# Attention output stored without padding, its denominators inverted where they are used and spread by TensorE

## The chip, the core and the metric

The kernel runs on one core of a Trainium2 chip. The metric is the device time of one execution in microseconds (us). The kernel before takes 3326.37 us, the median of three runs (3324.26 to 3327.92).

## The reference, cut to what matters

Eight batches of 512 tokens of width 256 pass through a cross-attention to a context of 1601 tokens, then through a block of causal self-attention and eight routed experts. The change touches how the output of both attentions is normalized:

```python
x = x + xattn(layernorm(x), ctx, ctx, Wq, bq, Wk, bk, Wv, bv, Wo, bo)
# inside xattn, 16 heads of 16 columns:
scores = einsum('bqhd,bkhd->bhqk', q, k) * scale
attn = softmax(scores, axis=-1)
out = einsum('bhqk,bkhd->bqhd', attn, v).reshape(B, -1, DIM)
return out @ Wo.T + bo
# then, with x <- layernorm(x):
h = x + attention(rmsnorm(x, g1), wq, wk, wv, wo)     # causal, 512 tokens, rotary
y = h + moe(rmsnorm(h, g2), w_router, wg, wu, wd)     # 8 experts, top 2
```

## The kernel before, in words

The kernel is a sequence of stages. Each stage is a block in which every engine runs its own list of instructions. Engines wait for each other through semaphores, and a barrier of all engines stands between two stages. The stages are: `prepare_weights`; `project_inputs`; `attention` over the context (names with `att_cross_`); `invert_denominators`; `project_self` (names with `slf_`); `attention` over the tokens themselves (`att_self_`); `invert_denominators` again; `finish_self` (names with `fin_`); then routing, scattering, the experts and the final sum.

In `attention`, a unit is four heads of one batch, so there are 32 units in each attention. A head takes 32 rows of the 128 partitions of `out_buf`: 16 rows of output, one row with the softmax denominator (row `HD` of the head, because the values carry a column of ones), and 15 unused rows. SyncE sends each unit's 128 rows to DRAM as one transfer (`send_out`, L597).

`invert_denominators` reads the 128 denominator rows back from DRAM (L856), takes their reciprocal on VectorE (L864) and writes them to the DRAM tensor `inverse` (L858). `load_attention_out` (L875, L878), called by the two later stages, then gathers a batch with six transfers: four bring two row groups for each half of `oT`, and two read `inverse` so that each head's row is repeated for its 16 partitions. VectorE multiplies the two in `divide` (L1040 and L1252), and TensorE multiplies the result with the output weights (`out_product`, L990 and L1222).

`project_self` and `finish_self` are software pipelines over the eight batches, written by `turns`: a list of parts with lags for each engine. In step t, an engine runs each part of its list in the order written, for batch t minus the part's lag. So the order within a step is fixed and an engine that waits in one part does not go on to the next.

In `project_self` the parts are: on VectorE `subtract_high` of k (L1078), `residual` (L1046, with the sums of the first norm), `divide` (L1040), `rope(0)` (L1070, L1071, which reads the products of q), `layer_norm` (L1052, L1056), `rms_inverse`, `subtract_high` of q and `rope(1)` (k). On TensorE they are `turn_rows` (L999, a transposition of the rows that ScalarE scaled after the layer norm), `out_product` (L990), `q_products` (L1008), `v_product` (L1022) and `k_products` (L1008). The products of q and k share PSUM banks, so `k_products` waits until `rope(0)` has read those of q. `residual` also waits until the rows of the batch before have landed in DRAM (`rows_sent`).

In `finish_self` every batch also loads two tensors of rows (L1209) and stores two (L1298, L1303). GpSimd's `weigh` (L1328) waits until the stored rows of the batch before have landed.

## Time and profile before

| what | value |
|---|---|
| median of three runs | 3326.37 us |
| the profiled execution, its own time | 3328.94 us |
| its span in the profile | 3327.4 us |
| busy PE, VectorE, ScalarE, GpSimd | 81%, 53%, 44%, 15% |
| mean granted TensorE clock | 0.905 |

The profile divides the span into stages that do not overlap, since a barrier ends each. A stage is as long as its own slowest chain, so a mean over the span tells little: TensorE is 81% busy over the whole, but 75% in `project_self` (180.91 us of 240) and 43% in `finish_self` (75.83 us of 175). The rows below are read stage by stage.

### The profile page before, as it was taken

What the parts mean: (1) busy time and instruction counts of PE and PEld (TensorE: products, weight loads), DVE (VectorE), ACT (ScalarE), POOL (GpSimd) and SP (SyncE); (2) the same over time, 40 slices, a digit from 0 to 9 for tenths busy, and PEclk for the clock granted to TensorE, in tenths of its full rate; (3) what the DMA queues carried; (4) which work ended last, traced back from release to release, by engine and by line L of the source; (5) the groups of instructions that cost most, each with busy time, mean ns of one, the idle gap of its engine ahead of it and who ended that gap; (6) DMA issues with size and microseconds to landing.
All of it is one profiled execution on the core that took longest, in us unless ns stands there. A gap on an engine that the chain in (4) does not pass through costs nothing. (4 is left out here: it accounts for less than half of the span.)

```text
span 3327.4 us, 54791 instructions
## 1 busy us (share of the span) xinstructions
PE 2706.5 (81%) x14654; PEld 1326.7 (40%) x14655; DVE 1767.8 (53%) x2838; ACT 1460.1 (44%) x2951; POOL 488.0 (15%) x638
## 2 busy tenths in 40 slices
PE   7996899999999999999948778888341299999980
PEld 5662232323232323233235434443231177777760
DVE  5665776767676767677346556664222022222223
ACT  2331576767676767677713335555110022222210
POOL 2444000000000000000014411110133400000006
PEclk9996899999999999999979979999665599999995
DMA  7888444444444444443045556654444211001115
GB/s 239 266 286 155 79 72 77 71 77 71 76 72 75 73 73 75 72 74 58 22 133 195 178 131 142 142 141 105 145 144 152 95 33 33 32 32 32 32 46 182
DMA packets 317615, 347.91 MB, mean 105 GB/s; under 512 B 37328, under 2 KB 262776, under 8 KB 317312
## 3 DMA queue, kind: packets, MB, share of 16 engines
q1 hardware_dynamic: 285584, 291.53, 38.6%
q0 software_dynamic: 11392, 37.76, 3.6%
q10 hardware_dynamic: 20464, 16.40, 1.6%
q8 instruction: 96, 1.57, 0.2%
q14 instruction: 79, 0.65, 0.1%
HBM read 206.22 MB, written 138.57 MB: 104 GB/s over the span
## 5 line engine op out<-in xcount | busy, mean ns | idle before, releaser
L727 DVE TENSOR_REDUCE att_cross_neg_max<-att_cross_ps_s 128x1 f32<-128x802 f32 x1024 | 965.6, 988 | 357.3 <-PE att_cross_ps_s L644 355.6
L798 ACT ACTIVATE att_cross_probs<-att_cross_ps_st 128x512 f32<-128x512 f32 (+1 forms) x1664 | 901.4, 599 | 401.0 <-PE att_cross_ps_st L663 388.4
L663 PE MATMUL att_cross_ps_st<-att_cross_q_pack,att_cross_k_pack 99*128 99x512 bf16 (+1 forms) x1664 | 575.3, 391 | 42.7 <-issue 33.8
L644 PE MATMUL att_cross_ps_s<-att_cross_k_pack,att_cross_q_pack 96*128 96x401 bf16 x2048 | 548.2, 351 | 70.1 <-DVE att_cross_neg_max L727 29.5
L678 PE MATMUL att_cross_ps_o<-att_cross_probs,att_cross_v_tiles 128*32 128x512 f32 (+1 forms) x3328 | 453.4, 618 | 1.0
L644 PEld LDWEIGHTS att_cross_ps_s<-att_cross_k_pack,att_cross_q_pack 96*128 96x128 bf16 x2048 | 177.1, 100 | 420.6 <-DVE att_cross_neg_max L727 204.5
L663 PEld LDWEIGHTS att_cross_ps_st<-att_cross_q_pack,att_cross_k_pack 99*128 99x128 bf16 (+1 forms) x1664 | 163.1, 100 | 421.2 <-ACT att_cross_probs L798 293.1
L727 DVE TENSOR_REDUCE att_self_neg_max<-att_self_ps_s 128x1 f32<-128x128 f32 (+3 forms) x512 | 236.5, 489 | 162.7 <-PE att_self_ps_s L647 159.7
L798 ACT ACTIVATE att_self_probs<-att_self_ps_st 128x256 f32<-128x256 f32 (+3 forms) x512 | 208.5, 441 | 156.8 <-PE att_self_ps_st L666 150.8
L1756 DVE COPY moe_hiddenT<-moe_ps_h 128x256 f32<-128x256 f32 x142 | 60.3, 424 | 297.2 <-PE moe_ps_h L1666 297.2
L644 PE MATMUL att_self_ps_s<-att_self_k_pack,att_self_q_pack 96*128 96x128 bf16 (+3 forms) x512 | 160.6, 316 | 56.4 <-DMA att_self_q_pack<-q_parts 25.1
L1720 ACT ACTIVATE moe_silu<-moe_ps_g 128x352 f32<-128x352 f32 x142 | 65.8, 463 | 301.0 <-PE moe_ps_u L1658 301.0
L1676 PE MATMUL moe_ps_y<-top_wd_sb,moe_hiddenT 128*128 (+1 forms) x852 | 196.0, 379 | 1.2 <-DVE moe_hiddenT L1757 1.2
L1658 PE MATMUL moe_ps_g<-top_wg_sb,moe_rowsT 128*128 x568 | 192.8, 462 | 0.0
L1658 PE MATMUL moe_ps_u<-top_wu_sb,moe_rowsT 128*128 x568 | 192.0, 461 | 0.0
L769 POOL CAST att_cross_neg_max_parts<-att_cross_neg_max_merged 128x16 bf16<-128x16 f32 x32 | 6.1, 192 | 1245.1 <-DVE att_cross_neg_max_merged L718 1245.1
L1676 PEld LDWEIGHTS moe_ps_y<-top_wd_sb,moe_hiddenT 128*128 128x128 f32 (+1 forms) x852 | 161.6, 190 | 35.3 <-issue 1.5
L663 PE MATMUL att_self_ps_st<-att_self_q_pack,att_self_k_pack 99*128 99x256 bf16 (+3 forms) x512 | 157.4, 310 | 17.3 <-DMA att_self_q_pack<-att_self_neg_max_rows 15.2
L1750 DVE TENSOR_TENSOR moe_hidden<-moe_ps_u,moe_silu 128x352 f32<-128x352 f32 x142 | 73.5, 517 | 159.3 <-ACT moe_silu L1720 159.3
L1828 POOL DMA_INDIRECT comb_row<-out_sorted,comb_index x64 | 62.1, 970 | 622.6 <-DVE comb_index L1838 603.4
L1658 PEld LDWEIGHTS moe_ps_u<-top_wu_sb,moe_rowsT 128*128 128x128 f32 x568 | 108.5, 191 | 60.7 <-issue 1.0
L678 PEld LDWEIGHTS att_cross_ps_o<-att_cross_probs,att_cross_v_tiles 128*32 128x32 f32 (+1 forms) x3328 | 66.6, 108 | 151.9 <-ACT att_cross_probs L798 113.9
(208 smaller groups left out, 2910.6 us busy)
## 6 DMA issues: line engine op xcount, KB each, us to landing
att_cross_k_pack<-k_parts SPq DMA_DIRECT2D x192, 200.1 KB, 9.5
v_rows<-in_v_pad SPq DMA_DIRECT2D x24, 1024.0 KB, 4.5
att_cross_v_tiles<-v_rows SPq DMA_DIRECT2D x32, 768.0 KB
k_parts<-in_part SPq DMA_DIRECT2D x72, 256.0 KB, 4.0
in_rows<-in_ctx_dram SPq DMA_DIRECT2D x24, 512.0 KB, 4.8
att_cross_q_pack<-q_parts SPq DMA_DIRECT2D x192, 64.0 KB, 10.0
att_self_k_pack<-k_parts SPq DMA_DIRECT2D x192, 64.0 KB, 3.2
att_self_q_pack<-q_parts SPq DMA_DIRECT2D x192, 64.0 KB, 3.6
```

Source lines behind the costliest of these rows:

```text
L644: last = nc.tensor.matmul(ps_s[bank][:, n, 0:w], qp[v.buf][0:SROWS, j, q * P:(q + 1) * P], kp[v.buf][0:SROWS, j, s:s + w], start=True, sto ...
L663: mm = nc.tensor.matmul(ps_st[bank_of_step[s]][0:rows, q0:SEQ], kp[u.buf][0:MROWS, j, t * P:t * P + rows], qp[u.buf][0:MROWS, j, q0:SEQ], ...
L678: nc.tensor.matmul(ps_o[j * VW:(j + 1) * VW, q0:SEQ], va[u.vbuf][0:rows, t, j * VW:(j + 1) * VW], pr[0:rows, (u.odd * STEPS + t * GH + j) ...
L727: nc.vector.tensor_reduce(nmax[v.odd][:, col, half:half + 1], ps_s[bank][:, 0:len(spans), 0:spans[0][1]], AX.XY, ALU.max, negate=True).the ...
L769: link(nc.gpsimd.tensor_copy(nm_parts[:, 0, :], full))
L798: nc.scalar.activation(pr[0:rows, (u.odd * STEPS + s) % RING, q0:SEQ], ps_st[bank_of_step[s]][0:rows, q0:SEQ], ACT.Exp).then_inc(exp_done, 1)
L1658: last = nc.tensor.matmul(ps[half][:, 0:HHALF], xT[t.par][:, i, :], wt[:, bass.ds(at, HHALF)], start=(i == 0), stop=(i == KC - 1))
L1676: last = nc.tensor.matmul(ps_y[:, :], hT[half][0:CW[c], c, :], wd[0:CW[c], bass.ds(at, DIM)], start=(half == 0 and c == 0), stop=(half == ...
L1720: nc.scalar.activation(sil[half][:, :], ps_g[half][:, 0:HHALF], ACT.Silu).then_inc(sil_ready, 1)
L1750: nc.vector.tensor_tensor(h[half][:, :], ps_u[half][:, 0:HHALF], sil[half][:, :], ALU.mult)\
L1756: nc.vector.tensor_copy(hT[half][:, 0:CH - 1, :], ps_h[half][:, 0:CH - 1, :])
L1828: pool.indirect_dma_start(out=r[g][k][c][:, :], out_offset=None, in_=out_sorted, in_offset=bass.IndirectOffsetOnAxis(ap=index[g][:, c, k:k ...
```

## The change

The rows of `out_rows` are stored without padding. For each unit, SyncE sends four transfers of 16 rows and one of the 4 denominator rows, to a DRAM tensor of their own, `den_rows`. The two stages `invert_denominators` are gone. `load_attention_out` becomes two transfers a batch: the 256 rows of output and the 16 rows of denominators.

In `project_self` and `finish_self`, VectorE inverts the 16 denominator rows (`invert`, a new part ahead of `residual`). TensorE multiplies a constant 16 by 256 matrix of zeros and ones with them (`spread_inverse`, a new part at the head of its list), so that each head's row stands on its 16 partitions in PSUM. `divide` reads this PSUM tile. In `project_self` the tile is `ps_o`, the one that `out_product` writes afterwards, so `spread_inverse` waits until `residual` of the batch before has read it, and `divide` moves behind `rope(0)`. In `finish_self` the tile is one of its own, `ps_b`. The constants become 256 columns wider.

```diff
 def send_out(v):
     sp.wait_ge(o_read, v.n + 2)
-    sp.dma_start(out_rows[v.n, :, :], ob[v.odd][:, :]).then_inc(o_sent[v.odd], 16)
+    for j in range(GH):
+        sp.dma_start(out_rows[v.batch, v.rows.start + j * HD:v.rows.start + (j + 1) * HD, :],
+                     ob[v.odd][j * VW:j * VW + HD, :]).then_inc(o_sent[v.odd], 16)
+    sp.dma_start(den_rows[v.batch, v.heads, :], ob[v.odd][HD:P:VW, :]).then_inc(o_sent[v.odd], 16)
...
+def load_attention_out(eng, out_rows, den_rows, oT, den, b, arrived):
+    eng.dma_start(oT[:, :, :], out_rows[b, :, :].rearrange("(c p) n -> p c n", p=P)).then_inc(arrived, 16)
+    eng.dma_start(den[:, :], den_rows[b, :, :]).then_inc(arrived, 16)
...
 # project_self, TensorE
+def spread_inverse(b):
+    pe.wait_ge(inv_ready, b + 1)
+    pe.wait_ge(x1_ready, b + 1)
+    for c in range(KC):
+        last = nc.tensor.matmul(ps_o[:, c * 2:(c + 1) * 2, :].rearrange("p t d -> p (t d)"),
+                                keep["spread"][0:HEADS, c * P:(c + 1) * P], inv[:, :],
+                                start=True, stop=True)
+    last.then_inc(spread, 1)
-turns(pe, batches, ((1, turn_rows), (0, out_product), (1, q_products), (1, v_product),
+turns(pe, batches, ((0, spread_inverse), (1, turn_rows), (0, out_product), (1, q_products), (1, v_product),
                     (1, k_products)))
 # project_self, VectorE
 def divide(b):
+    dve.wait_ge(spread, b + 1)
+    nc.vector.tensor_tensor(on[:, :, :], oT[:, :, :],
+                            ps_o[:, :, :].rearrange("p (c t) d -> p c (t d)", c=KC),
+                            ALU.mult).then_inc(on_ready, 1)
+def invert(b):
     dve.wait_ge(att_in, (b + 1) * ATT_LOADS)
-    nc.vector.tensor_tensor(on[:, :, :], oT[:, :, :], inv[:, :, :], ALU.mult).then_inc(on_ready, 1)
+    dve.wait_ge(spread, b)
+    nc.vector.reciprocal(inv[:, :], den[:, :]).then_inc(inv_ready, 1)
-turns(dve, batches, ((3, lambda b: subtract_high(1, b)), (1, residual), (0, divide),
-                     (2, lambda b: rope(0, b)), (1, layer_norm), (1, rms_inverse),
+turns(dve, batches, ((3, lambda b: subtract_high(1, b)), (0, invert), (1, residual), (2, lambda b: rope(0, b)),
+                     (0, divide), (1, layer_norm), (1, rms_inverse),
                      (2, lambda b: subtract_high(0, b)), (2, lambda b: rope(1, b))))
 # finish_self, TensorE and VectorE
-turns(pe, batches, ((2, turn_rows), (0, out_product), (2, router)))
+turns(pe, batches, ((0, spread_inverse), (2, turn_rows), (0, out_product), (2, router)))
-turns(dve, batches, ((1, residual), (0, divide), (1, mean_square), (1, rms_inverse),
+turns(dve, batches, ((0, invert), (1, residual), (0, divide), (1, mean_square), (1, rms_inverse),
                      (3, take_logits)))
```

VectorE, the body of the loop of `project_self` before, from the second instruction on. A row is a line of the code, the operation, what it writes and reads, and its shape.

```order
L1046 TENSOR_TENSOR slf_x<-slf_ps_o,slf_x_biased 128x1024
L173 BN_STATS slf_norm_stats<-slf_x 128x6 x4
L176 BN_AGGR slf_norm_mean_var<-slf_norm_stats 128x2 x4
L1040 TENSOR_TENSOR slf_o_normed<-slf_oT,slf_inv_rows 128x1024
L1070 TENSOR_TENSOR slf_rope_cos<-slf_ps_a,top_keep_constants 128x512
L1071 TENSOR_TENSOR slf_rope_sin<-slf_ps_b,top_keep_constants 128x512
L1052 RECIPROCAL slf_norm_std_inv<-slf_norm_std 128x4
L1056 TENSOR_SCALAR slf_h<-slf_x,slf_norm_mean_var,slf_norm_std_inv 128x256 x4
```

The same place in the changed kernel:

```order
L1031 RECIPROCAL slf_inverse<-slf_denominators 16x512
L1037 TENSOR_TENSOR slf_x<-slf_ps_o,slf_x_biased 128x1024
L173 BN_STATS slf_norm_stats<-slf_x 128x6 x4
L176 BN_AGGR slf_norm_mean_var<-slf_norm_stats 128x2 x4
L1061 TENSOR_TENSOR slf_rope_cos<-slf_ps_a,top_keep_constants 128x512
L1062 TENSOR_TENSOR slf_rope_sin<-slf_ps_b,top_keep_constants 128x512
L1024 TENSOR_TENSOR slf_o_normed<-slf_oT,slf_ps_o 128x1024
L1043 RECIPROCAL slf_norm_std_inv<-slf_norm_std 128x4
L1047 TENSOR_SCALAR slf_h<-slf_x,slf_norm_mean_var,slf_norm_std_inv 128x256 x4
```

A reciprocal of 16 rows of 512 has come in ahead of the residual, and the division has moved from ahead of the rope rows to directly ahead of the layer norm (L1043). It now reads `slf_ps_o`, a PSUM tile.

TensorE, the body of the loop of `project_self` before:

```order
L999 MATMUL slf_ps_t<-top_keep_constants,slf_x_rms 128x128 x8
L990 MATMUL slf_ps_o<-top_keep_WoT,slf_o_normed 128x256 x8
L1008 MATMUL slf_ps_a<-slf_xT,top_keep_wq 128x512 x4
L1008 MATMUL slf_ps_b<-slf_xT,top_keep_wq_rot 128x512 x4
L1022 MATMUL slf_ps_t<-top_keep_wv,slf_xT 128x256 x8
L1008 MATMUL slf_ps_a<-slf_xT,top_keep_wk 128x512 x4
L1008 MATMUL slf_ps_b<-slf_xT,top_keep_wk_rot 128x512 x4
```

And in the changed kernel:

```order
L965 MATMUL slf_ps_o<-slf_inverse,top_keep_constants 128x512 x2
L983 MATMUL slf_ps_t<-top_keep_constants,slf_x_rms 128x128 x8
L974 MATMUL slf_ps_o<-top_keep_WoT,slf_o_normed 128x256 x8
L992 MATMUL slf_ps_a<-slf_xT,top_keep_wq 128x512 x4
L992 MATMUL slf_ps_b<-slf_xT,top_keep_wq_rot 128x512 x4
L1006 MATMUL slf_ps_t<-top_keep_wv,slf_xT 128x256 x8
L992 MATMUL slf_ps_a<-slf_xT,top_keep_wk 128x512 x4
L992 MATMUL slf_ps_b<-slf_xT,top_keep_wk_rot 128x512 x4
```

Two matmuls (L965) stand at the head of the body, that is, behind the products of k of the step before.

## Rows read from the trace of the kernel before

**Rows 1.** Windows: stretch, length, busy PE, PEld, DVE, ACT, POOL, clock, DMA, GB/s.

```profile
1678.00:1918.00 240.00, 180.91 (x576) 106.99 (x576) 134.77 (x290) 70.92 (x129) 95.29 (x64) 0.90 0.53 175
2337.00:2512.00 175.00, 75.83 (x320) 64.65 (x320) 45.80 (x112) 24.97 (x49) 43.09 (x40) 0.65 0.45 144
```

**Rows 2.** Timeline (start, length, instruction, [idle before]) between the cross attention and `project_self`.

```profile
1663.89 0.33 SPq L597 DMA_DIRECT2D out_rows<-att_cross_out_buf  x1
...
1668.14 0.34 SPq L856 DMA_DIRECT2D inv_cross_den<-out_rows  x1
1670.84 3.35 DVE L864 RECIPROCAL inv_cross_inv<-inv_cross_den 128x512 f32<-128x512 f32 x1 [50.27 <-DMA inv_cross_den<-out_rows]
...
1677.28 0.91 DVE L1032 MEMSET slf_v_pad<- 128x1024 f32 x1 [3.10 <-PEq L65]
1678.34 1.29 SPq L875 DMA_DIRECT2D slf_oT<-out_rows  x2
```

**Rows 3.** Timeline of SyncE between the self attention and `finish_self`.

```profile
2327.37 0.35 SPq L856 DMA_DIRECT2D inv_self_den<-out_rows  x1
...
2336.80 1.26 SPq L875 DMA_DIRECT2D fin_oT<-out_rows  x2
```

**Rows 4.** Timeline of one step in the middle of `project_self`.

```profile
1795.15 1.23 DVE L1046 TENSOR_TENSOR slf_x<-slf_ps_o,slf_x_biased 128x1024 f32<-128x1024 f32 x1 [2.08 <-DMA h_rows<-slf_h]
...
1798.24 1.19 DVE L1040 TENSOR_TENSOR slf_o_normed<-slf_oT,slf_inv_rows 128x1024 f32<-128x1024 f32 x1
...
1799.35 0.68 DVE L1070 TENSOR_TENSOR slf_rope_cos<-slf_ps_a,top_keep_constants 128x512 f32<-128x512 f32 x1
...
1801.74 0.17 DVE L1052 RECIPROCAL slf_norm_std_inv<-slf_norm_std 128x4 f32<-128x4 f32 x1
...
1801.88 3.70 PE L1008 MATMUL slf_ps_a<-slf_xT,top_keep_wk 128*128 128x512 f32 x8 [1.67 <-DVE slf_rope_sin L1071]
...
1805.42 3.60 PE L1008 MATMUL slf_ps_b<-slf_xT,top_keep_wk_rot 128*128 128x512 f32 x8
...
1810.47 1.09 PE L999 MATMUL slf_ps_t<-top_keep_constants,slf_x_rms 128*128 128x128 f32 x8 [1.46 <-ACT slf_x_rms L1103]
...
1814.85 3.60 PE L1008 MATMUL slf_ps_a<-slf_xT,top_keep_wq 128*128 128x512 f32 x8
...
1816.98 1.22 DVE L1078 TENSOR_TENSOR slf_roped_rest<-slf_roped,slf_roped_part 128x1024 f32<-128x1024 f32 x1 [4.86 <-ACT slf_roped_part L1124]
...
1821.72 3.62 PE L1022 MATMUL slf_ps_t<-top_keep_wv,slf_xT 128*128 128x256 f32 x16
```

**Rows 5.** Timeline of `project_self`, its first division and products, first and last transposition.

```profile
1690.07 1.22 DVE L1040 TENSOR_TENSOR slf_o_normed<-slf_oT,slf_inv_rows 128x1024 f32<-128x1024 f32 x1 [11.60 <-DMA slf_inv_rows<-inverse]
...
1691.35 6.51 PE L990 MATMUL slf_ps_o<-top_keep_WoT,slf_o_normed 128*128 128x256 f32 x16 [28.21 <-DVE slf_o_normed L1040]
...
1712.05 1.97 PE L999 MATMUL slf_ps_t<-top_keep_constants,slf_x_rms 128*128 128x128 f32 x8 [14.19 <-ACT slf_x_rms L1103]
...
1882.69 1.09 PE L999 MATMUL slf_ps_t<-top_keep_constants,slf_x_rms 128*128 128x128 f32 x8 [0.76 <-ACT slf_x_rms L1103]
```

**Rows 6.** The division of `finish_self`: count, duration in ns (min/median/max), first and last start.

```profile
L1252 DVE TENSOR_TENSOR fin_o_normed<-fin_oT,fin_inv_rows x8: 1224/1226/2485, 2349.9 to 2475.5; 128x1024 f32<-128x1024 f32 x8
```

**Rows 7.** Timeline of `finish_self`, one load of the attention's output.

```profile
2351.32 1.40 SPq L875 DMA_DIRECT2D fin_oT<-out_rows  x2
...
2362.56 1.23 DVE L1252 TENSOR_TENSOR fin_o_normed<-fin_oT,fin_inv_rows 128x1024 f32<-128x1024 f32 x1 [4.12 <-DMA fin_inv_rows<-inverse]
```

**Rows 8.** Waits of `finish_self`: us in total, times, longest.

```profile
POOL fin_h_normed L1328 <- DMA hn_rows<-fin_h_normed: 84.8, 6, 20.1
```

**Rows 9.** The page's DMA issues: count, KB each, median us to landing.

```profile
in_rows<-in_ctx_dram SPq DMA_DIRECT2D x24, 512.0 KB, 4.8
```

**Rows 10.** Waits of SyncE in the self attention.

```profile
SPq L588 <- PE att_self_ps_o L678: 137.6, 28, 15.6
```

**Rows 11.** Timeline of SyncE in the self attention, one unit's store.

```profile
2112.01 0.38 SPq L597 DMA_DIRECT2D out_rows<-att_self_out_buf  x1
```

More of the change, by code:

```diff
@@ L448, in project_inputs, with attention @@
         p.clear()
-def attention(nc, q_parts, k_parts, v_rows, out_rows, kv, causal, keep, units, beside=None):
+def attention(nc, q_parts, k_parts, v_rows, out_rows, den_rows, kv, causal, keep, units, beside=None):
     tiles = [(t, min(P, kv - t * P)) for t in range(-(-kv // P))]
@@ L531, in __init__ @@
                 self.rows = slice(g * GR, (g + 1) * GR)
+                self.heads = slice(g * GH, (g + 1) * GH)
                 self.columns = slice(g * GH * VW, (g + 1) * GH * VW)
@@ L624, in _ @@
                 for k in range(2):
-                    sp.wait_ge(o_sent[k], 16 * (units // 2 + 1))
+                    sp.wait_ge(o_sent[k], OSENT * (units // 2 + 1))
             @block.tensor
@@ L912, in project_self @@
         on_ready = p.sem("on_ready")
+        inv_ready = p.sem("inv_ready")
+        spread = p.sem("spread")
         xb_ready = p.sem("xb_ready")
@@ L1183, in finish_self @@
         on_ready = p.sem("on_ready")
+        inv_ready = p.sem("inv_ready")
+        spread = p.sem("spread")
         o_done = p.sem("o_done")
@@ L1216, in _, with spread_inverse @@
                 pe.sem_inc(turned, 1)
+                def spread_inverse(b):
+                    pe.wait_ge(inv_ready, b + 1)
+                    pe.wait_ge(on_ready, b + 1)
+                    for c in range(KC):
+                        last = nc.tensor.matmul(ps_b[:, c, :],
+                                                keep["spread"][0:HEADS, c * P:(c + 1) * P], inv[:, :],
+                                                start=True, stop=True)
+                    last.then_inc(spread, 1)
                 def out_product(b):
@@ L1250, in divide, with invert @@
                 def divide(b):
+                    dve.wait_ge(spread, b + 1)
+                    nc.vector.tensor_tensor(on[:, :, :], oT[:, :, :], ps_b[:, :, :], ALU.mult).then_inc(on_ready, 1)
+                def invert(b):
                     dve.wait_ge(att_in, (b + 1) * ATT_LOADS)
-                    nc.vector.tensor_tensor(on[:, :, :], oT[:, :, :], inv[:, :, :], ALU.mult).then_inc(on_ready, 1)
+                    dve.wait_ge(spread, b)
+                    nc.vector.reciprocal(inv[:, :], den[:, :]).then_inc(inv_ready, 1)
                 def residual(b):
@@ L1867 @@
              ("cos_k", SEQ), ("sin_k", SEQ), ("iota_left", EXPERTS), ("iota_tile", 96), ("iota_count", 64),
-             ("lt8", EXPERTS * EXPERTS))
+             ("lt8", EXPERTS * EXPERTS), ("spread", DIM))
 def shape_constants():
@@ L1890, in shape_constants @@
         "lt8": np.tile((e[None, :] < e[:, None]).astype(np.float32).reshape(1, -1), (P, 1)),
+        "spread": (np.arange(DIM)[None, :] // HD == i[:, None]).astype(np.float32),
     }
@@ L1951, in build @@
     v2_rows = dram("v2_rows", [batches, SEQ, HEADS * VW])
[L1952 to L1953 removed]
+    out2_rows = dram("out2_rows", [batches, DIM, SEQ])
+    den2_rows = dram("den2_rows", [batches, HEADS, SEQ])
     tokens = batches * SEQ
```

68 lines of the change are left out of this document (19 added, 49 removed).

## The prediction

> **What bounds the kernel now.** I read the stages first. `project_self` and `finish_self` are two stretches of the span between barriers [rows 1], so what the change does there adds up with what it does at the two joins. The reader should see two different stages. In the first, TensorE is busy 181 of 240 us at a granted clock of 0.90. In the second it is busy 76 of 175 us at 0.65, with the 16 DMA engines at 0.45. Then I read the two joins [rows 2, 3], and last the timeline of one step of each pipeline.
>
> A step of `project_self` [rows 4]: the transposition for batch t-1 starts at 1810.47, its products of v at 1821.72, and the products of k run from 1801.88 to 1809.02. So TensorE goes round almost without a pause: it waits 1.5 us for the scaled rows and 1.7 us for VectorE's rope. From the first transposition to the last are 170.64 us for seven steps [rows 5], 24.4 us each. The point to see is what runs beside k: the division is done at 1799.4, the rope at 1801.8, and the layer norm starts at 1801.74. VectorE's and ScalarE's 8.7 us from there to the transposition lie under the 7.1 us of the products of k.
>
> A step of `finish_self` takes (2475.5 - 2349.9) / 7 = 17.9 us from division to division [rows 6]. All eight divisions end a wait for a load. One load, alone on the queues, takes 2362.56 - 2351.32 = 11.2 us [rows 7], though it moves 1 MB. GpSimd waits 84.8 us in six times for stored rows to land [rows 8].
>
> **Joins.** Both inversion stages go. At the first, the next stage's memsets can start where L856 stands (1668.14) and its first load 1.06 us later, against 1678.34 [rows 2]: 9.1 us less. At the second 9.4 us [rows 3]. Sum -18.6. Against it, the last unit's store is now five issues instead of one. At 0.38 us an issue [rows 11] that is 1.5 us later, for two stages +3.0. **Joins: -15.6 us**, bounds -18.6 (the four earlier ones hidden in the wait for the landing) and -12 (each issue doubled by its address arithmetic).
>
> In the attentions themselves, a unit gets four more issues on SyncE, 1.5 to 3 us. SyncE waits 137.6 us in 28 times for the values' buffer [rows 10], 4.9 us a unit, so they are hidden in the self attention, whose units are the short ones. If the issues took over 1.2 us each, the loads would come late. I take 0.
>
> The constants grow by 128 KB. By 512 KB in 4.8 us [rows 9] that is at most 1.2 us ahead of the first matmul. It is one more stream among others there. **+0.5 us.**
>
> **The steps of `project_self`.** This is the term that decides. `divide` for batch t now waits for `spread_inverse`, which stands on TensorE behind the products of k of the step before. The layer norm for t-1 stands behind `divide`, and the transposition for t-1 waits for the layer norm. What ran beside k now runs after it. I call D the start of a division, and work out the next D from rows 4.
>
> - D to the transposition: the division 1.2, then from the layer norm's start to the transposition 8.7, less the 0.8 us in which ScalarE was busy with a cast that is now long done: D + 9.1.
> - TensorE from there: products of v at + 11.25, hence k possible at + 14.7: D + 23.8.
> - k also needs the rope of q. VectorE reaches it after `subtract_high` at transposition + 6.5 (D + 15.6, 1.2 us), the new reciprocal, and the residual with its sums (3.1 us up to the rope). The reciprocal of 128x512 took 3.35 us [rows 2]. No row has 16 partitions. Its bounds are 0.2 (the 128x4 one took 0.17 us, rows 4) and 3.35, and I take 3.35, since the columns are the same 512. The rope then starts at D + 23.2, and k 2.5 us later, D + 25.7.
> - k takes 7.0 until TensorE is free, D + 32.7. The spread is two matmuls of 512 columns in fp32. Eight records of such are 3.6 us, and four matmuls are eight records, so two are 1.8 to 1.9. Next D = D + 34.6.
>
> The loads for batch t+1 are issued at D + 1.3 and needed at D + 16.8, and the stored rows have 11 us more than before, so no transfer ends a wait here. A step is 34.6 us instead of 24.4. The first transposition: the division for batch 0 came 11.7 us after the first load (1690.07, rows 5). Now 5.5 us of load, 3.35 of reciprocal and 3.6 of a spread at the low clock make 12.7, and the second round has the reciprocal and the spread in it again: 37.5 us after the first load instead of 33.7, +3.8. Six steps of 34.6 and a last one of 22.0, which has no division behind it, make 229.6 against 170.64: +59.0. Together **+62.8 us**. With the reciprocal at its lower bound k starts at D + 23.8 and the term is +51.
>
> **The clock.** TensorE now stands idle from the end of the spread to the transposition, 9.2 us in each step. After the idle 14.2 us before 1712.05 the granted clock was at its lower level: the transposition took 1.97 us instead of 1.09, and the cold product of 16 records 6.51 us [rows 5]. In `finish_self`, with pauses of similar length, the mean clock is 0.65 [rows 1]. Up to 9.2 us of each step at half speed would cost 4.6 us less what waits for the rope anyway (1.9), six times: 16 us, or 28 us if it falls on k. Nothing here shows a pause of 9 us behind 25 us of dense work. I take **+8 us**, bounds 0 and +28.
> The Trainium skill (TensorE: Matmul & The Clock Gate, section HAM oscillation) says that idle waits between groups of matmuls send the clock back to half in each group. By that rule the term would stand at the upper part of its range. The rows of `finish_self` agree with it.
>
> **The steps of `finish_self`.** The load becomes 0.5 MB in two transfers. The nearest row is 512 KB in 4.8 us [rows 9], so 11.2 becomes about 6. Behind it come the reciprocal, 3.35, and a spread at the low clock, 3.6, which stand in the chain from load to division: 13 us against 11.2 + 1.2. By this path alone nothing is won. But a step takes 17.9 us, since stored rows land late and the next loads wait for them behind GpSimd. A sixth of the bytes of a step goes (3.0 MB to 2.5 MB), and that shortens each landing. I take 16 us a step, **-14 us** for seven. Bounds: 13 us a step, -35, and 2 us a step more, +14.
> The Trainium skill (DMA: Bandwidth & Descriptors, section Queues, rings and completion order) says that a transfer runs on as many engines as divide the slowest dimension of both sides. The old gather's source had 4 there, the repeated one 8, the new load has 128. By that rule the old loads sat on four engines and held up every store behind them, and the term would be nearer to -35. No view of the trace before splits the engines.
>
> **Sum.** -15.6 + 0.5 + 62.8 + 8 - 14 = +41.7 us. The profiled execution took 3328.94 us (its span 3327.4 and 1.5 around it), 2.6 above the median, and would become 3370.6. On the median, 3326.4 + 41.7 = 3368.1 us.
>
> **The rivals.**
> 1. The steps of `project_self` do not grow. Then the joins and `finish_self` remain: -15.6 + 0.5 - 14 + 4 = -25, 3301 us. It needs the division to find its spread ready while k still runs. For it speaks that VectorE has 10 us of idle time in a step, so that 4 us more work fit. Against it stands TensorE's list: two matmuls cannot pass eight. A chance of 0.08. This is the one on the other side, and it decides from the point at which the spread comes before k.
> 2. The loads were the bound of everything: `finish_self` at -35, the reciprocal cheap (-11.8) and the clock unmoved: 41.7 - 21 - 11.8 - 8 = +1, 3327 us. A chance of 0.05.
> 3. The clock falls in every step and `finish_self` gains nothing: 41.7 + 20 + 14 = +76, 3402 us. A pause of 9 us in each step speaks for it, TensorE's 70% of busy time in a step against it. A chance of 0.08.
> 4. The change does not do what it says, the loads being no faster. The 0.5 MB then takes 11 us as before, and in `finish_self` 7 us of reciprocal and spread come on top of a step: 7 x 5 instead of -14: +91, 3417 us. Rows 9 speak against it. A chance of 0.03.
>
> My forecast, slower by the stretched step, has 0.76. The range is 3338 to 3398 us. The lower end is reached with the reciprocal cheap and `finish_self` at -26 together with a smaller clock term, the upper with the clock term at +28 and `finish_self` at -4. About 0.2 is left out on both sides. A difference of 0.2% (6.7 us) is what a measurement of this kernel can tell from none. Faster: rival 1 and a little of rival 2, 0.09. Same: the rest of rival 2 and a very cheap case of the forecast, 0.04. Slower: 0.87.
>
> **What would show it.** In the changed kernel, transpositions (L983) about 34.6 us apart, the two spread matmuls directly behind the products of k, a division that ends a wait for the spread in each step, and TensorE idle for 9 us behind it. `project_self` 300 to 315 us long. The joins 9 us shorter each. Divisions of `finish_self` about 16 us apart, their loads landing in about 6 us. The reciprocal of 16 rows at 3.35 us. The prediction is wrong if the transpositions stay within 27 us of each other, or if `finish_self` falls below 140 us.

## Result: 14 us slower, a third of what was forecast

The changed kernel takes 3338.6 us (median of five runs, 3336.3 to 3344.7), the kernel before, run beside it, 3324.3 us. The ratio is 1.005, with a 95% interval of 1.0035 to 1.0064, which is 12 to 21 us: slower by 14 us by the medians. The forecast was 42 us slower. The sign held, and so did the mechanism of `project_self`. Two terms of the sum were mis-sized, `project_self` by 15 us and `finish_self` by 17 us. One execution of `norm_and_store_first` (11080 us) and one of the kernel before beside it (6451 us) stand far outside all others and are left out of the ratios.

The profiled execution took 3344.66 us (span 3343.1), 6 us above the median. The stages are cut at the same instructions in both traces: the joins from the last copy of an attention's output to the next stage's first load, `project_self` from its first load to its last transposition, the self attention from its first load to its last copy, `finish_self` from its first load to the first reduction of the routing.

| part | before | after | difference | forecast |
|---|---|---|---|---|
| two joins | 15.05 + 14.04 | 8.12 + 6.54 | -14.4 | -15.6 |
| `project_self` | 204.35 | 259.97 | +55.6 | +62.8 + 8 |
| self attention | 403.11 | 412.49 | +9.4 | 0 |
| `finish_self` | 176.06 | 144.67 | -31.4 | -14 |
| all else | | | -3.5 | +0.5 |
| span | 3327.4 | 3343.1 | +15.7 | +41.7 |

The table compares one execution with one. The parts that the change decides, the joins, `project_self` and `finish_self`, give +9.8 us together.

The first join, SyncE in the timeline of the changed kernel:

```profile
1662.46 1.71 SPq L600 DMA_DIRECT2D out_rows<-att_cross_out_buf  x4
1664.21 0.52 SPq L602 DMA_DIRECT2D den_rows<-att_cross_out_buf  x1
...
1669.97 0.39 SPq L849 DMA_DIRECT2D slf_oT<-out_rows  x1
```

Against [rows 2] the inversion is gone and the first load stands 6.9 us closer to the last output. The five issues take 2.3 us instead of 0.33, 0.4 us more than forecast.

One step of `project_self`, TensorE and then VectorE, in the changed kernel:

```profile
1768.91 1.96 PE L983 MATMUL slf_ps_t<-top_keep_constants,slf_x_rms 128*128 128x128 f32 x8 [7.65 <-ACT slf_x_rms L1094]
1770.66 5.33 PE L974 MATMUL slf_ps_o<-top_keep_WoT,slf_o_normed 128*128 128x256 f32 x16
1775.83 3.60 PE L992 MATMUL slf_ps_a<-slf_xT,top_keep_wq 128*128 128x512 f32 x8
1779.27 3.60 PE L992 MATMUL slf_ps_b<-slf_xT,top_keep_wq_rot 128*128 128x512 f32 x8
1782.70 3.62 PE L1006 MATMUL slf_ps_t<-top_keep_wv,slf_xT 128*128 128x256 f32 x16
1786.15 3.60 PE L992 MATMUL slf_ps_a<-slf_xT,top_keep_wk 128*128 128x512 f32 x8
...
1793.11 1.98 PE L965 MATMUL slf_ps_o<-slf_inverse,top_keep_constants 16*128 16x512 f32 x4
```

```profile
1761.30 1.22 DVE L1024 TENSOR_TENSOR slf_o_normed<-slf_oT,slf_ps_o 128x1024 f32<-128x1024 f32 x1 [9.51 <-PE slf_ps_o L965]
...
1762.68 1.38 DVE L1047 TENSOR_SCALAR slf_h<-slf_x,slf_norm_mean_var,slf_norm_std_inv 128x256 f32<-128x256 f32 x4
...
1776.55 3.33 DVE L1031 RECIPROCAL slf_inverse<-slf_denominators 16x512 f32<-16x512 f32 x1
...
1795.13 1.22 DVE L1024 TENSOR_TENSOR slf_o_normed<-slf_oT,slf_ps_o 128x1024 f32<-128x1024 f32 x1 [9.65 <-PE slf_ps_o L965]
```

This is the chain that the prediction described, and it answers to [rows 4]. VectorE waits 9.65 us for the spread, then TensorE waits 7.65 us for the layer norm behind the division. From division to division are 33.8 us (34.1 in the last steps, 24.4 before). The windows show the clock: half of full speed for 10.2 us that begin within the pause, full speed in the rest of the step.

```profile
1764.30:1774.50 10.20, 5.59 (x18) 4.86 (x19) 5.67 (x16) 4.38 (x9) 4.43 (x2) 0.52 1.01 364
1774.50:1798.40 23.90, 20.59 (x59) 10.75 (x58) 12.92 (x23) 4.35 (x8) 7.16 (x6) 0.99 0.12 42
```

In `finish_self` the divisions are 14.7 us apart (17.9, [rows 6]), and one step reads:

```profile
2456.15 1.22 DVE L1256 TENSOR_TENSOR fin_o_normed<-fin_oT,fin_ps_b 128x1024 f32<-128x1024 f32 x1 [2.79 <-PE fin_ps_b L1217]
...
2458.25 0.34 SPq L850 DMA_DIRECT2D fin_denominators<-den_rows  x1
...
2463.82 3.34 DVE L1261 RECIPROCAL fin_inverse<-fin_denominators 16x512 f32<-16x512 f32 x1 [3.42 <-DMA fin_denominators<-den_rows]
2467.21 3.77 PE L1217 MATMUL fin_ps_b<-fin_inverse,top_keep_constants 16*128 16x512 f32 x4 [2.41 <-DVE fin_inverse L1261]
2471.02 1.22 DVE L1256 TENSOR_TENSOR fin_o_normed<-fin_oT,fin_ps_b 128x1024 f32<-128x1024 f32 x1 [2.79 <-PE fin_ps_b L1217]
```

That is a closed loop through one buffer: division, loads, reciprocal, spread, division. What surprised is how fast the rest became. Stored rows land in 4.5 and 5.1 us, before in 8.2 and 9.4 (count, KB each, median us from issue to landing, over the whole stage; first before, then after):

```profile
y_rows<-fin_y ACTq DMA_DIRECT2D x8, 512.0 KB, 8.2
hn_rows<-fin_h_normed ACTq DMA_DIRECT2D x8, 512.0 KB, 9.4
```

```profile
y_rows<-fin_y ACTq DMA_DIRECT2D x8, 512.0 KB, 4.5
hn_rows<-fin_h_normed ACTq DMA_DIRECT2D x8, 512.0 KB, 5.1
```

The DMA view shows what changed on the engines. Each fence is one view of 40 slices, busy tenths of the 16 engines above and GB/s below; first before (2455 to 2476), then after (2456 to 2476):

```profile
DMA  2225749999983201113459999975542222222210
GB/s 98 101 94 109 142 154 365 279 252 326 351 263 101 72 20 16 43 23 113 179 168 324 328 377 380 376 250 199 195 172 109 101 96 103 101 101 94 98 49 0
```

```profile
DMA  0006199999999999999000000000000006499999
GB/s 0 0 0 18 33 330 385 387 383 356 361 377 393 357 385 387 379 391 360 27 0 0 0 0 0 0 0 0 0 0 0 0 10 92 61 326 365 377 391 373
```

Before, both loads in the view end in a tail with the share at 0.2 and some 100 GB/s, a quarter of the 385 GB/s of full stretches, and ahead of the second tail stand 1.6 us at 0.5 and 172 to 199 GB/s. After, all of that is gone. The prediction had only the mean share of 0.45, which is 0.44 after.

### The profile page after: what moved, and what is told of

It is laid out like the page before. It is cut to its first block and busy times, and to the rows that moved or that the text cites. A ratio compares the mean times of both kernels' runs of the same rounds, so it can differ in the third digit from the quotient of the medians.

```text
span 3343.1 us, 55461 instructions
## 1 busy us (share of the span) xinstructions
PE 2764.0 (83%) x14718; PEld 1351.7 (40%) x14719; DVE 1795.0 (54%) x2852; ACT 1461.1 (44%) x2951; POOL 483.6 (14%) x638
## 5 line engine op out<-in xcount | busy, mean ns | idle before, releaser
L668 PE MATMUL att_cross_ps_st<-att_cross_q_pack,att_cross_k_pack 99*128 99x512 bf16 (+1 forms) x1664 | 574.2, 390 | 43.6 <-issue 34.6
## 6 DMA issues: line engine op xcount, KB each, us to landing
att_cross_q_pack<-q_parts SPq DMA_DIRECT2D x192, 64.0 KB, 10.2
```

Source lines behind the costliest of these rows:

```text
L668: mm = nc.tensor.matmul(ps_st[bank_of_step[s]][0:rows, q0:SEQ], kp[u.buf][0:MROWS, j, t * P:t * P + rows], qp[u.buf][0:MROWS, j, q0:SEQ], ...
```

## Experiments on the step of `project_self`

My theory: nothing runs beside k, because the layer norm stands behind a division that waits for the spread. The rivals: the spread's place behind k on TensorE, or the added work itself. Each ratio is to runs of the kernel before on the same chip, whose medians lie between 3316 and 3324 us. Where a kernel was executed once, only its profile is read, and no ratio is given.

**Layer norm ahead of the division (`dve_norm_first`).**

```diff
-  (0, divide), (1, layer_norm), (1, rms_inverse),
+  (1, layer_norm), (1, rms_inverse), (0, divide),
```

> The changed kernel, only VectorE's list in project_self altered: the division stands behind the layer norm of the batch before, not ahead of it. TensorE's list is untouched, the spread still stands behind the products of k. Theory (the stretched step comes from the layer norm standing behind a division that waits for the spread, so nothing runs beside k): the layer norm runs beside k again, the spread fills the end of that time, and a step of project_self falls from 33.9 to 26 to 28 us (7.1 us of k, 1.9 of spread more than the 24.4 of before); project_self loses 35 to 48 us, the whole kernel comes to 3291 to 3304 us and is faster than before (3324). The granted clock stays at its upper level through the steps. Rival (the spread's place behind the products of k on TensorE is what stretches the step, as the prediction put it with 'it decides from the point at which the spread comes before k'): the step stays above 31 us and the kernel above 3320 us. Second rival (the reciprocal and the residual behind it set the start of k): the step is 29 to 31 us.

Measured: 3320.9 us, ratio 0.9999 (0.9986 to 1.0013). The steps are 30 to 32.8 us, not 26 to 28. The pause before the transposition is gone, but a new one of up to 5.8 us stands before k:

```profile
1842.83 5.36 PE L992 MATMUL slf_ps_a<-slf_xT,top_keep_wk 128*128 128x512 f32 x8 [5.83 <-DVE slf_rope_sin L1062]
```

It comes behind this chain on ScalarE and VectorE:

```profile
1831.79 1.05 ACT L1115 CAST slf_roped_part<-slf_roped 128x1024 bf16<-128x1024 f32 x1 [5.58 <-DMA k_parts<-slf_roped_part]
```

```profile
1832.87 1.23 DVE L1069 TENSOR_TENSOR slf_roped_rest<-slf_roped,slf_roped_part 128x1024 f32<-128x1024 f32 x1 [6.51 <-ACT slf_roped_part L1115]
1834.01 3.33 DVE L1031 RECIPROCAL slf_inverse<-slf_denominators 16x512 f32<-16x512 f32 x1
```

The theory is right on what was late, and wrong on what is late next. It also had the clock stay up. Behind the new pause it falls again: the products of k into `ps_a` take 5.4 to 6.6 us instead of 3.6.

**SyncE's store of k ahead of the loads as well (`norm_and_store_first`).**

```diff
-turns(sp, ..., ((0, load), (4, store_k), ...
+turns(sp, ..., ((4, store_k), (0, load), ...
```

> The kernel dve_norm_first with SyncE's list in project_self altered in one place: the store of the parts of k (batch t-4) stands ahead of the loads, which wait for the division, not behind them. What it is to tell apart: in dve_norm_first a step took 31.5 to 32.8 us, since ScalarE's cast of k waited 5.6 us for k_parts to land, and VectorE's subtract_high, the reciprocal, the residual and the rope stood behind it, so that the products of k waited 5.8 us. Theory (SyncE's queue is the cause: its head waits for the division, which now comes 7 us later against the transposition, and five transfers stand behind it): with the store of k ahead, subtract_high runs some 3.7 us earlier and a step is 26.5 to 29 us, project_self loses 20 to 35 us against dve_norm_first (3321), the kernel 3287 to 3301 us. Rival (the transfers collide on the DMA engines whatever their order): the step stays above 31 us, the kernel within 6 us of 3321.

Measured: 3307.8 us, ratio 0.9972 (0.9958 to 0.9987), steps of 28.9 to 29.2 us. So SyncE's queue was the cause of 3 us: its first part waits for the division, and the stores stood behind it. k still waits 3.6 us for the rope, behind the reciprocal; in the last step, which has no reciprocal, it waits 0.8 us.

**The spread ahead of k (`pe_spread_first`).**

```diff
-turns(pe, ..., ((0, spread_inverse), (1, turn_rows), (0, out_product), (1, q_products), (1, v_product),
-                (1, k_products)))
+turns(pe, ..., ((0, spread_inverse), (2, k_products), (1, turn_rows), (0, out_product), (1, q_products),
+                (1, v_product)))
 # VectorE
-((3, subtract_high k), (0, invert), ...
+((0, invert), (3, subtract_high k), ...
```

> The changed kernel with TensorE's list in project_self turned: the spread for batch t+1 stands ahead of the products of k for batch t-1 and behind those of v (k has lag 2 and stands second). VectorE's reciprocal is moved to the head of its list, the division stays where the changed kernel has it. Theory (order): the spread fills the 1.7 us in which TensorE waited for the rope before, the division starts when the rope is done, the layer norm runs beside k; a step of project_self of 24.4 to 26.5 us instead of 33.9, the kernel at 3281 to 3296 us. Rival (the added reciprocal of 3.3 us on VectorE and the spread's 1.9 us each lengthen the step even so): 28 to 30 us a step, 3305 to 3317 us. If the work itself and not its order were the cause, the step would stay near 33.9 us and the time near 3338 us.

Measured: 3285.2 us, ratio 0.9883 (0.9868 to 0.9898), and all steps from the second on 25.3 us:

```profile
1806.47 1.09 PE L983 MATMUL slf_ps_t<-top_keep_constants,slf_x_rms 128*128 128x128 f32 x8 [1.48 <-ACT slf_x_rms L1094]
...
1821.26 1.98 PE L965 MATMUL slf_ps_o<-slf_inverse,top_keep_constants 16*128 16x512 f32 x4
```

The same instructions in another order are 53 us faster. The added work costs 0.9 us a step (25.3 against 24.4); the order cost the other 8.7. The run moves the reciprocal too, but that alone gives nothing: without any reciprocal the steps of the changed kernel stay at 34.1 us (`no_reciprocal`, below).

**The clock (`pe_filler`, `filler_reciprocal_first`).**

```diff
+def filler(b):   # TensorE, directly behind spread_inverse
+    ...                      # waits until ps_t is free
+    for k in range(7):
+        nc.tensor.matmul(ps_t[:, 0, :], keep["ident"][:, :], keep["cos_q"][:, :], start=True, stop=True)
```

> The changed kernel with seven more matmuls of 128x128 by 512 columns (a constant by the identity, into a PSUM tile that the next transposition overwrites) directly behind the spread in every step of project_self, about 0.9 us each at the upper clock, 6.3 us in all, in TensorE's pause of about 7.6 us. They add nothing to the result. Theory (the lower granted clock after the pause costs 2.2 us a step: transposition 1.97 instead of 1.09, first products at half speed): the granted clock stays at its upper level through the steps, the transposition takes 1.1 us, v starts 11.3 us after it instead of 13.5, a step is 31.5 to 32 us instead of 33.9, and the kernel is 12 to 16 us faster than the changed one, 3322 to 3327 us. Rival (the clock costs nothing, because what follows waits for the rope or for ScalarE): the step stays at 33.5 to 34.2 us, 3336 to 3341 us. Second rival: the extra matmuls themselves delay the transposition, the step grows to 35 us and more.

Measured: 3335.7 us, ratio 1.0048 (1.0032 to 1.0064), steps of 33.15 us. The granted clock is 1.00 in the whole step, yet only 0.9 us is won, since k then waits for the rope:

```profile
1793.30:1826.50 33.20, 30.16 (x91) 16.11 (x92) 18.27 (x38) 8.62 (x16) 11.60 (x8) 1.00 0.41 143
```

```profile
1883.70 3.70 PE L992 MATMUL slf_ps_a<-slf_xT,top_keep_wk 128*128 128x512 f32 x8 [1.67 <-DVE slf_rope_sin L1068]
```

`filler_reciprocal_first` adds to this that VectorE's `invert` stands first in its list.

> The kernel pe_filler (seven extra matmuls behind the spread in project_self, which keep the granted clock up) with VectorE's reciprocal moved ahead of subtract_high, into time in which VectorE waits. In pe_filler a step fell by only 0.9 us (33.15 instead of 34.06), since the products of k then waited 1.67 us for the rope. Theory (the lower clock costs 2.2 us a step and was hidden by the reciprocal in the rope's chain): k starts when v ends, 22.4 us behind the division instead of 24.1, a step is 31.4 to 31.9 us and project_self loses 10 to 13 us against pe_filler; the kernel 3320 to 3328 us. Rival (the clock's price is the 0.9 us seen): the step stays at 33.0 us and k still waits, for something else than the rope.

Measured: 3315.1 us, ratio 0.9999 (0.9987 to 1.001), steps of 31.21 us with no wait before k. So the lower clock delays TensorE by 2.9 us a step (34.06 less 31.21). Of these only 0.9 us count in the changed kernel, since the rope is late by itself as long as the reciprocal stands in its chain.

**Without the reciprocals (`no_reciprocal`).** Both are replaced by a copy of 16x4; the division by the denominators is left out.

> The changed kernel with both reciprocals of 16x512 replaced by a copy of 16x4 (0.2 us); the tile is set to one ahead of the loop, so the division by the denominators is left out of the result. In finish_self the theory is a loop through one buffer: division, issue of the loads (1.5 us), landing of the denominators (5.6), reciprocal (3.3), spread (3.8), division. Without the reciprocal a step falls from 14.7 to 11.5 us and the stage by 22 to 26 us. Rival (stored rows or rows loaded are the bound, GpSimd waits 9 to 10 us in each step for hn_rows): a step stays above 13.5 us. In project_self the products of k start when v ends (24.6 us behind a division) while the rope ends 0.5 us earlier, so the theory that TensorE and not the reciprocal sets the step gives 33.3 to 34.1 us a step, 33.9 before; the rival, the prediction's, that the rope sets it, gives 32 us or less. The kernel as a whole: 3310 to 3318 us.

Measured, one execution: the steps of `project_self` stay at 34.1 us, so TensorE's products of v, not the rope, set the start of k. `finish_self` falls only from 144.7 to 138.1 us, not by 22. Its divisions are 13.5 us apart on average, at the edge of the rival's case: GpSimd waits 51.6 us there for stored rows, so behind the loop they are close.

## Experiments on `finish_self`

**The same bytes in three shapes.** Each batch loads 512 KB more, into a tile that nothing reads.

```diff
+# fin_extra_plain
+sp.dma_start(extra[:, :, :], out_rows[b, :, :].rearrange("(c p) n -> p c n", p=P))
+# fin_extra_gather: 4 transfers
+src = out_rows[b, c * P:(c + 1) * P, :].rearrange("(j w) n -> j w n", w=VW)
+sp.dma_start(extra[u * GR:(u + 1) * GR, c, :], src[:, 0:HD, :])
+# fin_extra_repeat: 2 transfers
+src = den_rows[b, c * 8:(c + 1) * 8, :].unsqueeze(1).broadcast_to([8, HD, SEQ])
+sp.dma_start(extra[:, c, :], src)
```

> The changed kernel; in finish_self every batch loads 512 KB more, a second copy of its 256 rows of output, as one transfer of 128 partitions into a tile that nothing reads. The stage then moves as many bytes as before the change. Read from the trace's finish_self alone (144.7 us there in the changed kernel, 175.9 before; divisions 14.7 us apart, 17.9 before). Theory 'shape' (the old loads were slow because their transfers of a few long strides and repeated rows kept a few DMA engines busy and the rest idle; the changed kernel's shape is what gains): 512 KB spread over all 16 engines cost at most 1.4 us a step at 380 GB/s, a step is 14.7 to 16.3 us, finish_self 145 to 158 us. Rival 'bytes' (a sixth fewer bytes are what shortened every landing, as the prediction had it): the step comes back to 17 to 18 us, finish_self to 168 to 178 us.

> The changed kernel; in finish_self every batch loads 512 KB more in four transfers of 64 partitions whose source is four blocks of 16 rows with 16 rows between them, the old gather's shape, into a tile that nothing reads. Same bytes as the run with one plain extra load. Theory 'shape, by the gather': a stretch with the DMA share at 0.2 to 0.4 comes behind each load and the stores and rows behind it land late, a step is 17 to 20 us, finish_self 165 to 185 us. Rival 'bytes': the same step as with the plain extra load, within 0.5 us. Rival 'shape, but by the repeated rows alone': as the plain one, and only the run with repeated rows is slow.

> The changed kernel; in finish_self every batch loads 512 KB more in two transfers that repeat each of 8 denominator rows on 16 partitions, the shape of the old load of the inverses, into a tile that nothing reads. Same bytes as the run with one plain extra load. Theory 'shape': with eight rows as the outer dimension the transfers keep half of the DMA engines or fewer busy, a step is 16 to 19 us and finish_self 155 to 180 us, more than with the plain extra load. Rival 'bytes': the same as with the plain extra load, within 0.5 us a step.

Measured, one execution each: `finish_self` takes 155.2, 167.3 and 161.3 us, against 144.7 without. They ran on another chip than the changed kernel, but `project_self`, which they leave alone, took 259.8 to 260.4 us there against 260.0. The gather's DMA view (2438 to 2455) has the tail of the kernel before:

```profile
DMA  4814699999999999999962222222222210000000
GB/s 19 48 34 60 200 301 364 378 378 381 378 386 395 405 405 400 383 383 386 393 246 99 99 101 101 106 96 106 96 106 96 106 43 0 0 0 0 0 0 0
```

Bytes alone cost 10.5 us, the gather's shape 12.1 and the repeated rows' shape 6.1 us more at equal bytes. Both theories hold a share, and the shape has the larger. Nothing waits for these extra loads except the next of them and the end of the stage, so they price the load on the queues and not the wait for the load itself.

The landing of stored rows, however, is mostly a matter of bytes. With the plain load, which has no tail, it is nearly back where it was before the change:

```profile
y_rows<-fin_y ACTq DMA_DIRECT2D x8, 512.0 KB, 7.7
hn_rows<-fin_h_normed ACTq DMA_DIRECT2D x8, 512.0 KB, 8.3
```

With the gather it is 8.5 and 10.9 us, with the repeated rows 8.2 and 9.4.

The prediction cited the Trainium skill (DMA: Bandwidth & Descriptors) for this; the rule that the number of engines is the largest up to 16 that divides the slowest dimension of both sides stands there in the section Why a DMA increments its semaphore by 16 and not by 1. The trace agrees: with four blocks as the outer dimension, 100 of 385 GB/s at a share of 0.2.

**Denominators loaded early (`den_loaded_early`, on top of `pe_spread_first`).**

```diff
+def load_denominators(b):          # SyncE, own semaphore
+    sp.wait_ge(inv_ready, b)
+    sp.dma_start(den[:, :], den_rows[b, :, :]).then_inc(den_in, 16)
-turns(sp, ..., ((1, load_rows), (0, load_attention)))
+turns(sp, ..., ((0, load_denominators), (1, load_attention), (1, load_rows)))
```

> The kernel pe_spread_first, with finish_self altered: the denominators of batch t+1 are loaded as soon as the reciprocal of t has read the tile (their own semaphore), so that the reciprocal and the spread run while the rows of output are still coming; only the multiplication waits for these. Theory (the loop of a step is load, reciprocal, spread, division, 14.7 to 15.5 us): reciprocal and spread leave the loop, what is left is bounded by the stored rows (GpSimd's wait for hn_rows), since without the reciprocal the stage still took 138.1 us. finish_self 130 to 138 us instead of 145, the kernel 3268 to 3280 us. Rival (the stored rows are the bound already): finish_self stays at 142 to 146 us, the kernel at 3283 to 3288 us.

Measured: 3267.0 us, ratio 0.9855 (0.9837 to 0.9874); `finish_self` 134.5 us, against 145.0 in `pe_spread_first`. (From here on the stage's first load is that of the denominators. The expectations below count from the first load of output rows, 5.8 us later in this kernel: 128.7 us.) Reciprocal and spread have left the loop. GpSimd's wait for stored rows is now the largest:

```profile
POOL fin_h_normed L1344 <- DMA hn_rows<-fin_h_normed: 62.3, 7, 10.3
```

**That store issued earlier: first by ScalarE, then by SyncE.** `hn_stored_early` puts `store_normed` first in ScalarE's list. `hn_stored_by_sync` moves it to SyncE instead:

```diff
-((0, load_denominators), (1, load_attention), (1, load_rows))
+((0, load_denominators), (1, load_attention), (3, store_normed), (1, load_rows))
```

> The kernel den_loaded_early with ScalarE's list in finish_self altered: the store of the normalized rows of batch t-1 stands first in the step, not behind the norm of batch t. Theory (GpSimd waits 9 to 10 us a step for hn_rows to land because it is issued a step late, behind a norm that waits for the residual): the store starts as soon as the rows are there and lands before they are wanted, a step falls to 10 to 13 us and finish_self to 105 to 128 us, the kernel to 3245 to 3270 us. Rival (1.5 MB of loads and 1 MB of stores a step at some 380 GB/s, 6.9 us, and their latencies are the bound): no more than 3 us off finish_self against den_loaded_early.

> The kernel den_loaded_early with the store of the normalized rows in finish_self issued by SyncE between the load of the output rows and the load of the next rows, with lag 3, and no longer by ScalarE behind the norm of the next batch. In hn_stored_early the same store at the head of ScalarE's list made the stage 13.5 us longer, since ScalarE then waited there for GpSimd and took the turned rows late. Theory (the store is issued 4 us late in den_loaded_early, and GpSimd waits 10 us a step for its landing): issued by an engine whose next part waits for the same GpSimd instruction anyway, it delays nobody; a step falls from 12.5 to about 10.5 to 12 us, finish_self from 128.7 to 113 to 125 us, the kernel to 3254 to 3264 us. Rival (the loads of rows are held up behind it on the same queue, or DMA time is the bound): finish_self stays at 126 us or more, the kernel at 3265 us or more.

Measured: on ScalarE it misses, 3285.7 us, ratio 0.9901 (0.9878 to 0.9925), `finish_self` 148.1 us, 13.6 us longer. ScalarE waits there for GpSimd, takes the turned rows late, and TensorE's router, with the next spread behind it, waits for that:

```profile
PE fin_ps_l L1249 <- ACT fin_hT L1310: 28.0, 8, 4.4
```

On SyncE it is 3249.95 us, ratio 0.9806 (0.9784 to 0.9828), `finish_self` 118.1 us, 16.4 us shorter than in `den_loaded_early`. GpSimd no longer waits for a landing in this stage. This version beats both kernels, the one before by 64 us (57 to 72).

## Experiments on the store and on GpSimd's neighbour

**The five stores in the kernel before (`before_split_send`).**

```diff
-sp.dma_start(out_rows[v.n, :, :], ob[v.odd][:, :])
+for j in range(GH):
+    sp.dma_start(out_rows[v.n, j * VW:j * VW + HD, :], ob[v.odd][j * VW:j * VW + HD, :])
+sp.dma_start(out_rows[v.n, HD:P:VW, :], ob[v.odd][HD:P:VW, :])
```

> The kernel before, only send_out altered: each unit's output goes to its old place with the five transfers of the changed kernel (four of 16 rows, one of 4 rows) instead of one of 128; the 15 unused rows of each head are not sent. All else as before, the inversion through DRAM too. Theory (the self attention's 9.4 us more in the changed kernel come from these transfers): the self attention grows from 403 to 409 to 414 us, with PE's waits for the row maxima's transfer (neg_max_rows) up from 15 to about 22 us, the cross attention does not grow, and the kernel takes 3330 to 3336 us, 6 to 11 us more than before. Rival (the 9.4 us come from something else, the state in which project_self leaves the chip or chance in the clock's dips): the self attention stays at 401 to 405 us and the kernel within 3 us of before, up to 3 us slower by the later last store at each join. Second rival (SyncE's issue time holds up the loads of the next unit): growth with waits for q_parts or k_parts instead.

Measured: 3329.6 us, ratio 1.0018 (1.0009 to 1.0027), 3 to 9 us slower. The joins are 1.9 and 2.1 us longer, but the self attention takes 400.9 us, not 409 to 414. My theory fell, although the time came near what it gave. With the five stores the self attention took 400.4 to 407.2 us in thirteen other profiled executions. So the 9.4 us of the changed kernel's profile belong to that execution. The joins' 4 us lie within the interval of 3 to 9; whether the 2 us beyond them are real stays open.

**Why the layer norm became cheaper (`no_bias_rows`, on top of `dve_norm_first`).** GpSimd's bias addition is cut to 4 columns, which leaves the residual out.

> The kernel dve_norm_first with GpSimd's bias addition in project_self cut from 256 to 4 columns of each row tile (the rest of the tile is zero, so the residual of x and the bias are left out of the result). Theory (VectorE's layer norm runs at half speed or less while GpSimd adds the bias, the two sharing their way to memory; the changed kernel has its norm at another time and so gained 1.5 us a step that the prediction did not count): the four TENSOR_SCALARs of the layer norm take about 0.4 us each, 1.38 together, instead of 0.81 to 0.88 each, 3.25 together. Rival (they are slow beside the products of k or beside stored rows, whatever GpSimd does): they stay above 2.5 us together. A part of the slowness may stay, since another GpSimd addition (roped) comes earlier into the same time: then 1.4 to 2.3.

Measured, one execution: the four TENSOR_SCALARs take 4.10 us, longer, not shorter:

```profile
1841.42 4.10 DVE L1047 TENSOR_SCALAR slf_h<-slf_x,slf_norm_mean_var,slf_norm_std_inv 128x256 f32<-128x256 f32 x4
```

```profile
1842.28 0.75 POOL L1137 TENSOR_TENSOR slf_x_biased<-slf_x_rows,top_keep_bo 128x4 f32<-128x4 f32 x4
1842.99 2.39 POOL L1143 TENSOR_TENSOR slf_roped<-slf_rope_cos,slf_rope_sin 128x1024 f32<-128x1024 f32 x1
```

The rope's addition had moved under the norm, so the run does not tell what the norm costs without GpSimd. The other traces do. In the sixteen profiled executions the norm takes 1.38 us whenever GpSimd computes nothing beside it, and 2.2 us or more whenever it does. Taken one by one, the instructions show how. In the last step of the changed kernel, VectorE and GpSimd:

```profile
1921.80 2.41 DVE L1047 TENSOR_SCALAR slf_h<-slf_x,slf_norm_mean_var,slf_norm_std_inv 128x256 f32<-128x256 f32 x1
```

```profile
1921.71 2.35 POOL L1141 TENSOR_TENSOR slf_roped<-slf_rope_cos,slf_rope_sin 128x1024 f32<-128x1024 f32 x1 [2.20 <-DVE slf_rope_sin L1062]
```

The first TENSOR_SCALAR ends 0.15 us after the addition, and the next three take 0.40 us each. Beside the four short bias additions of the kernel before, the two engines take turns, and the later three TENSOR_SCALARs take 0.81 us each, 2.85 in all. That is read from the traces after the fact; no run took GpSimd away altogether.

## Why the prediction was right in sign and wrong in size

The measured 3338.6 us stand at the lowest edge of the range of 3338 to 3398, and the difference is a third of the forecast one. Two steps of the sum failed: the chain of `project_self` up to the first products of k, and "a sixth of the bytes of a step goes" in `finish_self`.

- Joins: right, -14.4 against -15.6.
- "A step is 34.6 us instead of 24.4": 34.1 in the last steps. The mechanism is as described, and `pe_spread_first` shows rival 1's condition, that the gain comes when the spread stands before k. The mis-sized term is "D to the transposition: ... D + 9.1". It took 7.6 us, since I carried over the layer norm's 2.85 us from a time when GpSimd computed beside it; here it took 1.38. 34.6 less 1.5 is 33.1, and with the clock kept up `pe_filler` measured 33.15. Over six steps: -9 us.
- "k also needs the rope of q": right at a full clock (24.1 us behind the division in `pe_filler`, 25.7 less 1.5). In the changed kernel v ended last, at 24.6, since the clock delayed it past the rope. The reciprocal, 3.33 us, was priced rightly.
- The first transposition came 32.4 us after the first load, not 37.5: the two loads landed in about 4 us, not 5.5, and the norm was shorter. -5 us. (The forecast's own terms for the first division add up to 12.5 us, not 12.7. It took 11.5.)
- The clock, "I take +8 us": 0.9 us net in six steps, and 2.4 in the last (25.07 against 22.67 with the filler), together 7.9. It did fall in every step, as rival 3 said, but most of it lay beside the rope's wait, as the sum had it ("less what waits for the rope anyway"). That the total came out at the 8 that I took is luck: I chose it between 0 and 28, for six steps, and almost a third of it fell in a seventh. What remains of the stage's 15 us are -1.1: the last step takes 22.7 without the clock, not 22.0, and the first steps were 1.8 us shorter than the later ones.
- The forecast also gave `project_self` as 300 to 315 us. From its first load to that of the self attention it takes 297.5 us, before 241.3.
- `finish_self`, "I take 16 us a step": 14.7, -23.0 us in seven, and 2.0 us less before the first division and 6.4 less behind the last, where I had counted nothing. Here the step that failed is "a sixth of the bytes of a step goes". By the three runs with extra loads, one execution each, the bytes were a third of the effect (10.5 of 31.4 us), and the shape of the transfers most of the rest (12.1 and 6.1). That fewer bytes shorten each landing was right. That they are all that changes was not: I had cited the rule on the engines and gave it no weight, because no view splits the engines. The DMA view over 20 us does show it.
- The self attention, 0: right over many executions, though one profile shows +9.4.
- The parts that the change decides add up to +9.8 us, and the interval of the measured difference is 12 to 21. The 2 us or more between them are not placed. In the stages that the change leaves alone, single executions differ by more than that: from the routing to the end they take 804 to 815 us.

## What to carry to other kernels

In a fixed order on each engine, count what runs beside the longest product before and after. If a new wait moves a chain out from under it, the whole chain is paid, however small the added work, and turning the order gives it back. When something is moved, look at what is queued behind the new wait on every engine, SyncE and ScalarE included. Before pricing a transfer by its bytes, look at the DMA view in short windows: a share of 0.2 at 100 GB/s is a shape, not a load.

## What the runs showed of the hardware

- A reciprocal goes by its columns: 16x512 took 3.33 us, 128x512 3.35.
- Transfers whose source has four blocks as its outer dimension ran at 100 GB/s with the DMA share at 0.2, stretches with transfers of 128 partitions at 385. At equal bytes they made `finish_self` 12.1 us longer.
- Stores of 512 KB from ScalarE's queue landed in 4.5 and 5.1 us. With 512 KB more to load in each step they landed in 7.7 and 8.3 us (plain), 8.2 and 9.4 (repeated rows), 8.5 and 10.9 (gather).
- A TENSOR_SCALAR of VectorE that met a running TENSOR_TENSOR of GpSimd ended 0.15 us after it: 2.41 us instead of 0.40. The Trainium skill (SBUF — State Buffer, section SBUF: two separate sides) calls the port pair that the two engines share an exclusive lock, held for the whole instruction. The trace agrees.
- A pause of 7.65 us in each step of 34 put the clock to half for 10.2 us. TensorE was busy in 26.2 of the 34.1 us. In the same kernel with extra matmuls in the pause it stayed at full. Behind a pause of 5.8 us (`dve_norm_first`) the first products were slow too, 5.4 us instead of 3.6.
